# Reordered TensorE steps in the second attention layer, a store on another queue in the third, and eight buffers in the target pass of a four-layer GNN kernel

## What is computed

```python
edge_index = jnp.stack([src, dst])
h = jnp.maximum(_layernorm(x, axis=-1), 0.0)
x = x + _L0_gnn_ref(h, edge_index, edge_weight1, ...)   # two GATv2 layers (8 heads x 16, 2 heads x 64), then an MLP
h = jnp.maximum(_layernorm(x, axis=-1), 0.0)
x = x + _L1_gnn_ref(h, edge_index, ...)                 # one attention layer, softmax over the source
h = jnp.maximum(_layernorm(x, axis=-1), 0.0)
x = x + _L2_gnn_ref(h, node_type_2, src, dst, ...)      # one matrix per kind of edge
h = jnp.maximum(_layernorm(x, axis=-1), 0.0)
x = x + _L3_gnn_ref(h, edge_index, edge_attr_16, ...)   # one GATv2 layer (4 heads x 16), batch norm, gelu
return x
```

```python
z = leaky_relu(xl[src] + xr[dst] + ee)
score = einsum('ehc,hc->eh', z, att)
a = exp(score - segment_max(score, dst)[dst])
out = segment_sum(xl[src] * a, dst) / segment_sum(a, dst)
```

## Time and profile before

| | us |
|---|---|
| Runs | 9160.83, 9188.93, 9189.82 (median 9188.93) |
| Profiled execution | 9215.03 (its span 9213.2) |
| DVE busy | 6495.0 (70%) |
| POOL busy | 4503.7 (49%) |
| PE busy | 4455.8 (48%) |
| ACT busy | 2837.8 (31%) |
| Mean granted clock of TensorE | 0.656 of full speed |

### The profile page before, as it was taken

The page is one execution under the profiler, slowest core; times in us unless marked ns, Lnnn a source line. Parts: engine busy times, 40 slices in busy tenths (PEclk is TensorE's granted clock), DMA queues, the critical chain, the costliest instruction groups (busy, mean ns, idle before and its releaser), DMA issues. The chain is left out here.

```text
span 9213.2 us, 91644 instructions
## 1 busy us (share of the span) xinstructions
PE 4455.8 (48%) x13072; PEld 2477.6 (27%) x13072; DVE 6495.0 (70%) x20579; ACT 2837.8 (31%) x6952; POOL 4503.7 (49%) x4361
## 2 busy tenths in 40 slices
PE   0000556565566565776000988867756676720000
PEld 0000222222233333665000546623323333310000
DVE  4227789888576776877566998767868787878422
ACT  0000344443122222555343000134434444457200
POOL 3760666664666664554554000055445565623566
PEclk9999766666677766555555997578865555555555
DMA  5000333334333331111453002566634444433222
GB/s 150 1 1 4 73 78 84 79 79 69 74 73 73 72 74 41 36 36 46 88 100 81 1 4 83 146 109 128 127 79 88 88 92 84 94 99 123 74 79 74
DMA packets 910191, 686.98 MB, mean 75 GB/s; under 512 B 599695, under 2 KB 748972, under 8 KB 909450
## 3 DMA queue, kind: packets, MB, share of 16 engines
q1 hardware_dynamic: 515806, 377.81, 15.5%
q0 software_dynamic: 137984, 138.92, 12.0%
q10 hardware_dynamic: 256232, 168.62, 5.9%
HBM read 491.06 MB, written 227.24 MB: 78 GB/s over the span
## 5 line engine op out<-in xcount | busy, mean ns | idle before, releaser
L755 POOL DMA_INDIRECT a_xg<-t_XL,c_at x784 | 808.5, 1031 | 741.9 <-issue 292.6
L755 POOL DMA_INDIRECT g_xg<-t_D,c_at x784 | 784.2, 1000 | 630.8 <-DMA t_HN<-g_hn 305.9
L755 POOL DMA_INDIRECT b_xg<-t_H,c_at x784 | 815.5, 1040 | 494.1 <-issue 242.8
L1740 POOL DMA_INDIRECT f_dg<-t_D,c_at x392 | 371.3, 947 | 1286.7 <-POOLq L175 974.3
L1088 POOL DMA_INDIRECT t_RANK<-m_place,m_at x392 | 386.2, 985 | 393.9 <-DMA m_place<-t_POS 285.8
L1273 POOL DMA_INDIRECT l_d<-t_D,l_ix x392 | 387.8, 989 | 318.4 <-DVE l_xs L1289 136.8
L403 POOL DMA_INDIRECT t_XL<-su_pos,su_scatx x392 | 405.1, 1033 | 245.2 <-DMA t_XL<-in_nodes 126.1
L2108 POOL DMA_INDIRECT out<-o_y,o_ix x392 | 385.9, 984 | 260.7 <-issue 209.5
L539 PE MATMUL su_bk<-c_ident,su_key 128*128 128x128 f32 x56 | 15.6, 434 | 847.9 <-DVE su_tmp L336 847.9
L1010 PE MATMUL g_bank<-g_zt,c_att3r 64*128 64x512 f32 x196 | 200.1, 1123 | 414.1 <-DVE g_zt L800 238.1
L1322 ACT ACTIVATE l_hn<-l_xs,l_sm 128x64 f32<-128x64 f32 x784 | 265.0, 426 | 429.1 <-DVE l_sm L631 348.0
(11 more groups left out here) (422 smaller groups left out, 15074.4 us busy)
## 6 DMA issues: line engine op xcount, KB each, us to landing
a_start<-t_START SPq DMA_DIRECT2D x98, 256.0 KB
t_XSD<-a_xg SPq DMA_DIRECT2D x98, 256.0 KB
t_H<-a_oE ACTq DMA_DIRECT2D x98, 256.0 KB
b_start<-t_START SPq DMA_DIRECT2D x98, 256.0 KB
l_xb<-t_XSD SPq DMA_DIRECT2D x49, 512.0 KB
f_rl<-t_REL SPq DMA_DIRECT2D x49, 512.0 KB
g_xb<-t_XSD SPq DMA_DIRECT2D x98, 256.0 KB
g_start<-t_START SPq DMA_DIRECT2D x98, 256.0 KB
```

The source lines that it names most:

```text
L755: nc.gpsimd.indirect_dma_start(xg[k][:, j, i, :], None, table, bass.IndirectOffsetOnAxis(ap=C["at"][:, i, n * J + j:n * J + j + 1], axis=0 ...
L1740: nc.gpsimd.indirect_dma_start(dg[k][:, u, j, :], None, T["D2"], bass.IndirectOffsetOnAxis(ap=C["at"][:, 0, (2 * n + u) * J + j:(2 * n + u ...
```

## The change

Three things are altered, and no instruction of the computation is added or left out.

1. In `b`, PE's step is now scores(n), project(n+1), turn(n+2), results(n-1), where it was project(n), scores(n), turn(n+1), results(n-1). ACT's `features` and `turned` are one chunk further ahead as well.
2. In `g`, the store of X3 goes from ACT's queue to SP's (`keep_sums`, lag 3). It and the reload of `g_xb` wait for a new semaphore `x3`, which DVE's add increments; DVE itself waits for that one in place of a link of its chain `ch1`. The store of HN3 keeps ACT's queue with semaphores of its own (`s_hst`), for which ACT's relu waits and POOL's gather no longer does. The load of `g_em` goes from lag 2 to 4.
3. In `o`, `SL` is 8, so that each of the eight tiles and its semaphores has eight buffers.

```diff
@@ gat_block
+            s_hst = m.sems("hst", SL)
...
-        NXST = 16 if tag == "a" else 32
+        NXST = 16
...
             def stored(n, k, q, old):
                 if old:
-                    hold(sp, S["spturn"], (S["hn"], n - SL + 1))
+                    hold(sp, S["spturn"], (S["x3"], n - SL + 1))
...
+            def keep_sums(n, k, q, old):
+                hold(sp, S["spturn"], (S["x3"], n + 1))
+                sp.dma_start(rows(T["X3"], n), xg[k][:, :, 1, :]).then_inc(s_xst[k], 16)
...
-                flow(sp, [(0, stored), (1, extras), (1, starts), (2, masks)], slots=SL)
+                flow(sp, [(0, stored), (1, extras), (1, starts), (3, keep_sums), (4, masks)], slots=SL)
...
-            ch1 = Chain(dve, S["ch1"], 1 + LN_OPS + (tag == "g"))
+            ch1 = Chain(dve, S["ch1"], 1 + LN_OPS)
...
-                    ch1(v.tensor_tensor(xg[k][:, :, :, :], xg[k][:, :, :, :], xb[k][:, :, :, :], ALU.add))
+                    v.tensor_tensor(xg[k][:, :, :, :], xg[k][:, :, :, :], xb[k][:, :, :, :], ALU.add
+                                    ).then_inc(S["x3"], 1)
+                    dve.wait_ge(S["x3"], n + 1)
...
                     if tag == "g":
-                        act.wait_ge(s_xst[k], NXST * q)
+                        act.wait_ge(s_hst[k], 16 * q)
...
-                    act.dma_start(rows(T["X3"], n), xg[k][:, :, 1, :]).then_inc(s_xst[k], 16)
-                    act.dma_start(rows(T["HN3"], n), hn[k][:, :, 1, :]).then_inc(s_xst[k], 16)
+                    act.dma_start(rows(T["HN3"], n), hn[k][:, :, 1, :]).then_inc(s_hst[k], 16)
...
             if wide:
-                stages = [(L, features), (L - 1, turned), (L, exponents), (L + 2, results)]
+                stages = [(L - 1, features), (L - 2, turned), (L, exponents), (L + 2, results)]
...
-            stages = [(L, project), (L, scores), (L - 1, turn), (L + 1, results)]
+            if wide:
+                stages = [(L, scores), (L - 1, project), (L - 2, turn), (L + 1, results)]
+            else:
+                stages = [(L, project), (L, scores), (L - 1, turn), (L + 1, results)]
@@ targets_block
-        SL = 4
+        SL = 8
```

More of the change, by code:

```diff
@@ L689, in gat_block @@
         s_ps = m.sem("ps")
-        names = "sq bs bc ln hn hT h z zs zt xl s ed ex den rec sum o div oE turn pturn spturn clear chz ch1 ch3 ch4 tail at"
+        names = "x3 sq bs bc ln hn hT h z zs zt xl s ed ex den rec sum o div oE turn pturn spturn clear chz ch1 ch3 ch4 tail at"
         S = {n: m.sem(n) for n in names.split()}
@@ L953, in _ @@
                     act.wait_ge(s_xst[k], NXST * chunks_of(k, SL))
+                if tag == "g":
+                    act.wait_ge(s_hst[k], 16 * chunks_of(k, SL))
             if tag == "a":
```

## The result

The change makes the kernel slower: 9254.43 us (median of 7 runs, 9222.42 to 9265.02) against 9188.93, a ratio of 1.0069 with an interval of [1.0054, 1.0084]. The forecast was 9040 us, in a range of 8920 to 9150. The profiled execution took 9255.20 us (span 9253.4), 40 us over the one before.

What follows compares the result with a forecast made beforehand. No engine was held to bound the whole kernel: a loop through `xl` bound `b`, DVE `g`, and POOL waited for loads in `o`. -90 + 0 - 60 = -150 us gave 9040 us at the median, range 8920 to 9150.

Steps and rivals of the forecast that it cites:

- The change in `g`: Third GAT layer: moving X3's store to SP's queue was taken to gain 0 us, bounds -30 to +20.
- POOL's 305.9 us: In `g`: POOL's wait filed under a store of HN, read as back pressure from late marks.
- The expected sign: In `g`: the span stays at 1391 us within 30, X3 is issued by SPq, no L903.
- slower: In `b`: POOL never halts and every handoff becomes late, +10.8 us per such chunk; 9233 us in all, chance 0.08.
- The change in `b`: Second layer: copying `xl` a chunk earlier lets POOL bind and gains 90 us, bounds 0 and -170.
- The loop: In `b`: L795 and L796, PE's scores, turn, results, next projections, ACT's copy, L795 again; 10.9 us a chunk.
- the term that I took off: In `b`: 27 of 30 late marks stay at 3 us each, 80 us off the 170 to be had.
- That gathers would grow above 1100 ns: Sign of being wrong: gathers, at a mean of 1040 ns in `b`, grow above 1100 ns.
- the Trainium skill's rule on contention: In `b`: a denser DVE lengthens gathers by 0.1 us a chunk, 10 us in all; the rows gave no such trend.
- The change in `o`: Target pass: eight buffers let SP load seven chunks ahead and gain 60 us, bounds -105 and 0.
- the 60% of the 102 us of waiting: In `o`: share of POOL's waiting between first and last scatter taken as gone, giving -60 us.
- only `b` gains: Rival: SP's issue binds `o` with eight buffers or four, so only -90 us comes: 9100 us, chance 0.12.

Runs made afterwards that it cites:

- the run with the old release: The changed kernel with the gather of `g` again waiting for HN3's store, X3's store left on SP: ratio 0.9919 to the kernel before, `g` 1281.3 us.
- four later releases in the same kernel: The changed kernel, POOL's gather in `g` released by HN3's store, DVE's next add, PE's turn or ACT's copy: ratios 0.9919, 0.9937, 0.9943, 0.9921.

## Why the prediction was wrong

**The step that failed** is "The change in `g` ... Taken: 0. Bounds: -30 to +20". It cost +136 us in the trace and 147 us alone. I had read POOL's 305.9 us in the earlier trace rows rightly as back pressure, and concluded that their releaser was of no account. But a wait that costs nothing also places the work behind it. The two stores held POOL back for some 4 us after `hn`, and this put its next burst where most of DVE's norm was done before marks got late. Released by `hn`, each burst starts some 3 us earlier against the norm, the last norm steps fall 8 us into it, `hn` is late and releases the next burst: the delay renews itself. I looked for the cost of the moved store (ACT's 0.55 us, SP's order), and the run with the old release (1281.3 us against 1284.4) shows that this part is nothing. The expected sign, a span of 1391 us within 30, failed with 1533. That the release decides is shown by four later releases in the same kernel; why a mark is late there stays open. The rival "slower" had the right effect, late handoffs of DVE as in the earlier trace rows, and the wrong place: `b`, at 10.8 us a chunk. It happened in `g`, at 15.6 - 12.1 = 3.5 us in the median chunk and 1.4 us in the mean one.

**The change in `b`** was forecast at -90 and gave -82 (24 us in a job where it started from 1184). That -90 and -82 are near is luck, since another term filled the place of the one that I had. The loop is cut, as said: DVE's idle time ahead of `b_zt` fell from 373.5 to 69.3 us,

```profile
L802 DVE TENSOR_TENSOR b_zt<-b_xl,b_bank 128x512 f32<-128x512 f32 x98 | 66.9, 683 | 69.3 <-issue 35.5 <-remote 19.2 <-ACT b_xl L925 14.6
```

and POOL's wait for the turn is nearly gone. But the term that I took off, 80 us of late marks, was mostly another. The late marks are still there (101.1 us "remote" ahead of DVE's L850, 143.5 us ahead of `b_xl` on ACT), but POOL hardly waits for them: it has 21.3 us of such waits. POOL did become the bound; its gathers became 90 ns longer each, 784 x 0.09 = 70 us, and 1063 + 70 = 1133 is all but 18 us of the 1150.7. That gathers would grow above 1100 ns was named as a sign of being wrong, and at 1130 it came. I had weighed the Trainium skill's rule on contention ("SBUF — State Buffer", Who interferes with whom: a DVE instruction with two SBUF inputs against a GpSimd instruction that reads SBUF), put it at 10 us, and found no trend in the earlier trace rows. The rows compare two stages by their averages, which hide what stands beside each gather. In the changed kernel:

```profile
2835.50 1.28 DVE L829 TENSOR_TENSOR_SCAN b_den<-b_ex,b_den 128x512 f32<-128x512 f32 x1
2835.82 1.72 POOL L760 DMA_INDIRECT b_xg<-t_H,c_at  x1 [4.53 <-remote]
...
2836.70 0.67 DVE L839 TENSOR_TENSOR b_msg<-b_ex,b_xl 128x512 f32<-128x512 f32 x1
2837.40 1.28 DVE L842 TENSOR_TENSOR_SCAN b_num<-b_ex,b_num,b_msg 128x512 f32<-128x512 f32 x1
2837.84 1.60 POOL L760 DMA_INDIRECT b_xg<-t_H,c_at  x1 [0.30 <-issue]
...
2839.74 0.94 POOL L760 DMA_INDIRECT b_xg<-t_H,c_at  x1 [0.30 <-issue]
...
2840.08 0.69 DVE L818 TENSOR_TENSOR b_ed<-b_bank,b_r 128x512 f32<-128x512 f32 x1
...
2843.70 0.69 DVE L857 TENSOR_TENSOR b_heads<-b_bank,b_recT 128x512 f32<-128x512 f32 x1
2843.73 0.94 POOL L760 DMA_INDIRECT b_xg<-t_H,c_at  x1 [0.30 <-issue]
```

The gathers beside L829, L839 and L842, which read two tiles in SBUF, take 1.72 and 1.60 us, those beside L818 and L857, with one input in PSUM, 0.94. From 2600 to 3200 us, 142 of 407 gathers took over 1.1 us. Laid over DVE's timeline, each has 1.53 us of DVE's work beside it on average, and none of that is L803, L818, L857 or L860, which are 0.40 of the 0.56 us beside a shorter one; L829, L839, L842, L819 and L820 are 1.23 of the 1.53. L817, with one tile in SBUF and one in PSUM, occurs beside both. The run with L812 and L813 on PSUM took these two out of the list. So the trace agrees with the rule, with one exception: L803 (`b_zt` twice, in SBUF) and L860 (both halves of `b_heads`) read SBUF for both inputs, and the gathers beside them have a median of 944 ns.

**The change in `o`** was forecast at -60 and gave -22, -13 to -20 alone. The mis-sized term is the 60% of the 102 us of waiting. SP does not wait for a buffer any more, and the slow issues go on, as the case "only `b` gains" had it. The quick loads run on in the pause and into the burst that POOL begins at 8841.14, then:

```profile
8845.68 0.39 SPq L2083 DMA_DIRECT2D o_h<-t_HN  x1
8846.17 0.38 SPq L2083 DMA_DIRECT2D o_x<-t_X  x1
...
8851.90 0.69 SPq L2083 DMA_DIRECT2D o_x<-t_X  x1
8854.74 1.40 SPq L2083 DMA_DIRECT2D o_ix<-t_SCAT  x1
8857.60 0.00 SPq L2083 DMA_DIRECT2D o_ag<-t_AG  x1
...
8865.36 0.70 SPq L2083 DMA_DIRECT2D o_ix<-t_SCAT  x1
8868.85 0.70 SPq L2083 DMA_DIRECT2D o_ag<-t_AG  x1
```

From 8851.90 the gaps are 2.8 and 2.9 us, and behind two shorter ones 5.6 and 3.5. The reserve of eight only makes a burst longer; later in it issue is slower than the 2.1 us that I had from bursts of five chunks. The Trainium skill's Key Constraints ("Trainium Kernel Development and Optimization") say that issuing from several engines only saves the sequencer's issue time. They say nothing of the pace of one queue while another issues, so they do not speak against a slow SP, as I had put it. In these rows issue itself slows on SP's queue while POOL issues, and in the run with two loads on ACT's queue it does so there (gaps of 2.1, 4.3 and 2.1 us from 8733.65 on).

## What to carry to other kernels

A wait on an engine that is ahead costs nothing by itself, but it sets when the work behind it starts, against the other engines. Before it is removed, lay the timelines of the engines over one another for a chunk or two and ask what the released work will then run beside. Chains of short steps on one engine, each waiting for the mark of the last, did best in these runs in the first four microseconds of a burst of gathers.

## What the runs showed of the hardware

- In `g` of the changed kernel POOL issues eight gathers on end, 1.25 us apart. The mark from one DVE instruction to the next is on time for the first six us of such a burst, and late from then on, by 1.3 us at most. The wait ahead of a norm step, marks of other engines among them, is 0.00 us on average in the first six us, 0.62 at 8 to 10 us and still 0.40 in the pause behind. A release about 1 us later took 71 us off the stage (1431.4 us with the edit alone, 1360.4 with the wait for PE's turn, on one chip in two jobs; `g` with the untouched release was 1257 to 1282 in the first job and 1296 to 1321 in the second).
- Why is not settled. It is not which rows are gathered. In the run with a pause in the chunk's middle 598 norm steps came 8 to 10 us into a burst and waited 0.00 us, which time alone does not explain.
- A gather in `b` of the changed kernel takes 0.94 us beside a DVE step with one input in SBUF and one in PSUM (L818, L857), and 1.20 to 1.69 us (medians) beside L819, L820, L829, L839 or L842, which read two SBUF tiles.
- SP's and ACT's DMA issues slow down in a burst, too. In `o` of the changed kernel, where SP waits for no buffer, its issues are 0.5 us apart at first and up to 7.8 us apart later (8823.80 to 8831.56), and half the issues on each of two queues do not bring the gaps down.
- The same kernel took 9062 to 9189 us (medians) in different jobs, and `b` with the old order 1183 to 1233 us. A part of what an edit gains in such a stage depends on that.
